# Two arrays in place of one for the sum of the experts' rows, in a graph and mixture-of-experts kernel

## What is computed

```
x = x + gnn0(layernorm(x))        # graph attention, 8 heads
x = x + ffn0(layernorm(x))        # 8 experts, each takes its 256 best nodes
x = x + gnn1(layernorm(x))        # mean over in-edges, two 512x512 products, silu
x = x + ffn1(layernorm(x))        # 64 experts, top 2 per node, plus a shared one

def ffn0(x_flat):                                  # E = 8, C = 256
    probs = softmax(x_flat @ Wr, axis=0)           # over the nodes
    vals, idx = top_k(probs.T, C)
    h = gelu(einsum('ecd,edf->ecf', x_flat[idx], W1) + b1[:, None, :])
    out_e = einsum('ecf,efd->ecd', h, W2) + b2[:, None, :]
    weighted = vals[..., None] * out_e
    return zeros_like(x_flat).at[idx.reshape(-1)].add(weighted.reshape(-1, D))
```

## Time and profile before

| What | Value |
|---|---|
| time, median of 3 runs | 2386.32 us (2380.95 to 2394.46) |
| profiled execution, its own time | 2389.54 us |
| its span, first to last instruction | 2387.8 us |
| mean granted TensorE clock | 0.941 |
| busy: PE, DVE, ACT, POOL | 84%, 59%, 43%, 43% of the span |
| moved by DMA | 537.31 MB, 225 GB/s over the span |

### The profile page before, as it was taken

The page is one execution under the profiler, slowest core; times in us unless marked ns, Lnnn a source line. Parts: engine busy times, 40 slices in busy tenths (PEclk is TensorE's granted clock), DMA queues, the critical chain, the costliest instruction groups (busy, mean ns, idle before and its releaser), DMA issues. The chain is left out here.

```text
span 2387.8 us, 35619 instructions
## 1 busy us (share of the span) xinstructions
PE 2007.8 (84%) x8691; PEld 1271.1 (53%) x8691; DVE 1417.0 (59%) x3001; ACT 1020.1 (43%) x3220; POOL 1021.7 (43%) x1046
## 2 busy tenths in 40 slices
PE   5857888888887725169999999897999999999998
PEld 4745667666665213124433444354346888888544
DVE  6646889888888662466666656577852222222343
ACT  2225777777776503456666556344001111111000
POOL 1037777777772404257777777300001111111331
PEclk9978999999999858679999999999999999999999
DMA  5648888888883735777777777785316999999652
GB/s 147 124 154 244 243 245 240 240 248 243 242 236 108 264 108 106 196 247 224 224 225 224 224 224 224 249 279 176 128 48 221 365 366 368 364 367 351 237 189 89
DMA packets 276215, 537.31 MB, mean 225 GB/s; under 512 B 43508, under 2 KB 121948, under 8 KB 275860
## 3 DMA queue, kind: packets, MB, share of 16 engines
q0 software_dynamic: 80544, 261.97, 37.9%
q1 hardware_dynamic: 177043, 240.65, 29.7%
q10 hardware_dynamic: 18464, 32.84, 4.2%
HBM read 449.56 MB, written 86.57 MB: 225 GB/s over the span
## 5 line engine op out<-in xcount | busy, mean ns | idle before, releaser
L852 POOL DMA_INDIRECT g_G<-tab,src_of_item x440 | 441.1, 1002 | 179.7 <-issue 106.7
L917 PE MATMUL g_psA<-g_G,g_oh 128*128 128x261 f32 x1760 | 443.0, 398 | 60.1 <-DVE g_G L1067 47.2
L1222 PE MATMUL g_psA<-g_G,g_oh 128*128 x832 | 386.0, 607 | 78.6 <-SPq L1178 69.5
L1162 POOL DMA_INDIRECT g_G<-tab,src_of_tile x392 | 370.7, 946 | 165.3 <-issue 84.1
L974 ACT ACTIVATE g_G<-g_G 128x64 f32<-128x64 f32 x1760 | 425.1, 336 | 0.0
L1265 DVE TENSOR_TENSOR acc<-acc,g_psA 128x512 f32 x416 | 285.5, 686 | 185.7 <-PE g_psA L1222 143.0
L917 PEld LDWEIGHTS g_psA<-g_G,g_oh 128*128 128x128 f32 x1760 | 326.7, 194 | 122.5 <-DVE g_G L1067 59.1
L1222 PEld LDWEIGHTS g_psA<-g_G,g_oh 128*128 128x128 f32 x832 | 147.3, 190 | 294.7 <-issue 293.8
L2427 PE MATMUL mo_bank<-mo_xT,mo_w 128*128 128x128 f32 x2304 | 269.1, 275 | 0.2 <-ACT mo_xT L2464 0.2
L2330 POOL DMA_INDIRECT mo_g<-tab,mo_slot x72 | 68.0, 945 | 456.9 <-PE mo_bank L2417 325.1
L2427 PEld LDWEIGHTS mo_bank<-mo_xT,mo_w 128*128 128x128 f32 x2304 | 263.0, 192 | 1.0 <-ACT mo_xT L2464 0.5
(11 more groups left out here) (421 smaller groups left out, 2524.4 us busy)
## 6 DMA issues: line engine op xcount, KB each, us to landing
mo_w<-in_L_ffn_w SPq DMA_DIRECT2D x216, 512.0 KB, 8.4
ys<-mo_y ACTq DMA_DIRECT2D x72, 256.0 KB, 5.6
g_ot<-reld SPq DMA_DIRECT2D x27, 512.0 KB, 5.9
ys<-sg_zeros SPq DMA_DIRECT2D x24, 512.0 KB, 4.2
g_G<-tab,src_of_item POOLq DMA_INDIRECT x440
g_pen<-pend SPq DMA_DIRECT2D x216, 32.0 KB
tab<-fi_row SPq DMA_DIRECT2D x25, 261.0 KB, 2.7
xmid<-at_x SPq DMA_DIRECT2D x25, 256.0 KB, 5.3
```

The costliest lines, as they stand in the source:

```text
L852: q.indirect_dma_start(G[:, j % RING, :], None, tab0, bass.IndirectOffsetOnAxis(K.src[:, j:j + 1], 0)).then_inc(gs[g % 3], 16)
L917: ins = tens.matmul(psA[u][:, f, 0:HW], oh[:, n % OR, h, :], G[:, r + h, f * HW:(f + 1) * HW], start=(h == 0), stop=(h == SUP - 1))
L1162: g.indirect_dma_start(G[:, (j + 1) % MR, :], None, table, bass.IndirectOffsetOnAxis(K.src1[:, j:j + 1], 0)).then_inc(got[j % MR], 16)
L1222: tens.matmul(psA[n % MB][:], oh[:, n % MO, :], G[:, ds(tile1 % MR, 1), :].rearrange("p o d -> p (o d)"), start=True, stop=True).then_inc( ...
```

## The change

The experts' rows are added into two arrays. Experts 0, 2 and 4 add into `xmid`, experts 1, 3, 5, 6 and 7 into a new array `xpart`, which `phase_route0` fills with zeros. Each array has its own chain of scatters with its own semaphore. `y` gets four buffers. SP loads the tiles of `xmid` when the first chain has landed, and the tiles of `xpart` through four buffers (`rest`) when the second has. POOL adds the two tile by tile, and VectorE's statistics wait for this (`joined`). `xmid` in memory keeps the first part alone, so `phase_sage` loads both arrays again for the residual, and POOL adds them there too (`whole`).

```diff
-def phase_route0(nc, K, lg, tab1, a, ew):
+def phase_route0(nc, K, lg, tab1, a, ew, xpart):
...
+        blank = p.sb("blank", [P, D])
...
         def _(g):
+            nc.gpsimd.memset(blank[:], 0.0).then_inc(blanked, 1)
             nc.gpsimd.iota(tio[:], [[1, NT], [0, E0]], base=0, channel_multiplier=0,
...
             loaded = ew.load(s, a, ws)
+            s.wait_ge(blanked, 1)
+            s.dma_start(xpart.rearrange("(t p) d -> p t d", p=P),
+                        blank[:].unsqueeze(1).to_broadcast([P, NT, D])).then_inc(bs, 16)
+            s.wait_ge(bs, 16)
             s.wait_ge(st, 16)
             s.wait_ge(ws, loaded)
...
-def phase_experts0(nc, K, a, tab1, xmid, ew, acc, tab2):
+def phase_experts0(nc, K, a, tab1, xparts, ew, acc, tab2):
...
+    YB = 4
+    ZB = 4
+    parts = ((0, 2, 4), (1, 3, 5, 6, 7))
+    part = [next(k for k in range(2) if e in parts[k]) for e in range(E0)]
+    rank = [parts[part[e]].index(e) for e in range(E0)]
...
-        y = p.sb("y", [P, 2, HC, D])
+        y = p.sb("y", [P, YB, HC, D])
+        rest = p.sb("rest", [P, ZB, D])
...
         def _(s):
-            s.wait_ge(sca, 16 * HC * E0)
+            s.wait_ge(sca[0], 16 * HC * len(parts[0]))
             for n in range(NT):
-                s.dma_start(xm[:, n, :], xmid[n * P:(n + 1) * P, :]).then_inc(xl[n], 16)
+                s.dma_start(xm[:, n, :], xparts[0][n * P:(n + 1) * P, :]).then_inc(xl[n], 16)
+            s.wait_ge(sca[1], 16 * HC * len(parts[1]))
+            for n in range(NT):
+                wait(s, joined, n - ZB + 1)
+                s.dma_start(rest[:, n % ZB, :], xparts[1][n * P:(n + 1) * P, :]).then_inc(rl[n % ZB], 16)
...
                 q.wait_ge(yr, HC * (e + 1))
-                if e:
-                    q.wait_ge(sca, 16 * HC * e)
+                k = part[e]
+                if rank[e]:
+                    q.wait_ge(sca[k], 16 * HC * rank[e])
                 for c in range(HC):
                     j = e * HC + c
-                    q.indirect_dma_start(xmid, bass.IndirectOffsetOnAxis(ix[:, j:j + 1], 0), y[:, e % 2, c, :], None,
-                                         bounds_check=NP - 1, compute_op=ALU.add).then_inc(sca, 16)
-            q.wait_ge(sca, 16 * HC * E0)
+                    q.indirect_dma_start(xparts[k], bass.IndirectOffsetOnAxis(ix[:, j:j + 1], 0), y[:, e % YB, c, :], None,
+                                         bounds_check=NP - 1, compute_op=ALU.add).then_inc(sca[k], 16)
+            for n in range(NT):
+                q.wait_ge(xl[n], 16)
+                q.wait_ge(rl[n % ZB], 16 * (n // ZB) + 16)
+                nc.gpsimd.tensor_tensor(xm[:, n, :], xm[:, n, :], rest[:, n % ZB, :], ALU.add).then_inc(joined, 1)
+            for k in range(2):
+                q.wait_ge(sca[k], 16 * HC * len(parts[k]))
...
-                    wait(v, sca, 16 * HC * (e - 1))
-                    nc.vector.tensor_tensor(y[:, e % 2, c, :], psY[c][:], b2[:, e, :], ALU.add).then_inc(yb, 1)
+                    if e >= YB:
+                        v.wait_ge(sca[part[e - YB]], 16 * HC * (rank[e - YB] + 1))
+                    nc.vector.tensor_tensor(y[:, e % YB, c, :], psY[c][:], b2[:, e, :], ALU.add).then_inc(yb, 1)
             for n in range(NT + 1):
                 if n < NT:
-                    v.wait_ge(xl[n], 16)
+                    v.wait_ge(joined, n + 1)
                     ln.stats(v, n, n % 2, xm[:, n, :])
...
-def phase_sage(nc, K, a, acc, own, xmid, tab3, ys, s13, s2, top, tix):
+def phase_sage(nc, K, a, acc, own, xmid, xpart, tab3, ys, s13, s2, top, tix):
...
+        xb = p.sb("xb", [P, XB, D])
...
             nc.gpsimd.memset(zeros[:], 0.0).then_inc(zr, 1)
+            for n in range(NT):
+                q_.wait_ge(xl[n % XB], 32 * (n // XB) + 32)
+                nc.gpsimd.tensor_tensor(xt[:, n % XB, :], xt[:, n % XB, :], xb[:, n % XB, :], ALU.add).then_inc(whole, 1)
...
                     s.dma_start(xt[:, n % XB, :], xmid[n * P:(n + 1) * P, :]).then_inc(xl[n % XB], 16)
+                    s.dma_start(xb[:, n % XB, :], xpart[n * P:(n + 1) * P, :]).then_inc(xl[n % XB], 16)
...
-                    v.wait_ge(xl[m % XB], 16 * (m // XB) + 16)
+                    v.wait_ge(whole, m + 1)
                     vv.tensor_tensor(acc[:, m, 0:D], sg[:, m % 2, :], xt[:, m % XB, :], ALU.add).then_inc(xd, 1)
```

More of the change, by code:

```diff
@@ L227, in build @@
     xmid = dram("xmid", [NP, D])
+    xpart = dram("xpart", [NP, D])
     tab1 = dram("tab1", [NP, D + E0])
@@ L256, in build @@
                 with ew:
-                    phase_route0(nc, K, lg, tab1, a, ew)
-                    phase_experts0(nc, K, a, tab1, xmid, ew, acc, tab2)
+                    phase_route0(nc, K, lg, tab1, a, ew, xpart)
+                    phase_experts0(nc, K, a, tab1, (xmid, xpart), ew, acc, tab2)
         best = sb("best", [P, NT, 8])
@@ L265, in build @@
                 phase_mean(nc, K, tab2, acc, a, own, s13, s2)
-                phase_sage(nc, K, a, acc, own, xmid, tab3, ys, s13, s2, best, tix)
+                phase_sage(nc, K, a, acc, own, xmid, xpart, tab3, ys, s13, s2, best, tix)
             phase_moe(nc, K, a, xmid, tab3, xsh, ys, own, s13, s2, best, tix, out)
@@ L1526, in phase_route0 @@
     with Phase(nc, "r0") as p:
+        blank = p.sb("blank", [P, D])
+        blanked = p.sem("blanked")
+        bs = p.sem("bs")
         pv = p.sb("pv", [P, 1])
@@ L1745, in phase_experts0 @@
     AHEAD = 4
+    YB = 4
[3 more added lines that the diff above has]
+    rank = [parts[part[e]].index(e) for e in range(E0)]
+    assert sorted(parts[0] + parts[1]) == list(range(E0))
     with Phase(nc, "e0") as p:
@@ L1751, in phase_experts0 @@
         hT = p.sb("hT", [F0, 2, CAP0])
-        y = p.sb("y", [P, 2, HC, D])
+        y = p.sb("y", [P, YB, HC, D])
+        rest = p.sb("rest", [P, ZB, D])
         ln = Norm(p, nc)
         normed = p.sem("normed")
+        rl = [p.sem(f"rl{q}") for q in range(ZB)]
+        joined = p.sem("joined")
         xl = [p.sem(f"xl{n}") for n in range(NT)]
@@ L1761, in phase_experts0 @@
         got = [p.gather_sem(f"got{e}") for e in range(E0)]; turned = p.sem("turned"); cop = p.sem("cop")
-        hd = p.sem("hd"); act = p.sem("act"); yd = p.sem("yd"); yb = p.sem("yb"); yr = p.sem("yr"); sca = p.gather_sem("sca")
+        hd = p.sem("hd"); act = p.sem("act"); yd = p.sem("yd"); yb = p.sem("yb"); yr = p.sem("yr"); sca = [p.gather_sem(f"sca{k}") for k in range(2)]
         b = p.block(K.counted)
@@ L1830, in _ @@
                     j = e * HC + c
-                    nc.scalar.activation(y[:, u, c, :], y[:, u, c, :], ACT.Copy,
+                    nc.scalar.activation(y[:, e % YB, c, :], y[:, e % YB, c, :], ACT.Copy,
                                          scale=g[:, j, D + e:D + e + 1]).then_inc(yr, 1)
@@ L1921, in phase_sage @@
         xl = [p.sem(f"xl{q}") for q in range(XB)]
+        whole = p.sem("whole")
         turned = p.sem("turned")
```

## The result

The changed kernel takes 2406.34 us (median of 5 runs, 2403.36 to 2408.47) against 2386.32; the ratio, taken over all runs, is 1.007, 95% interval 1.0055 to 1.0086. (The medians alone are 20.0 us apart; the five runs of before spread from 2380.95 to 2395.56.) It is slower, by more than the 0.5% that I had called the limit. The forecast was 2394.9 with a range of 2384 to 2406, and "same" had the largest chance: the sign of the sum was right, its size was half of what came. The median lies 0.3 us above the range; 2386.32 times the ratio, 2403.0, lies inside it. The profiled execution took 2406.47 us with a span of 2404.7, 16.9 us more than before.

The account below looks back on a forecast made before the run. Scatters of the experts' rows, then load, norm and store of the sum, were taken to bound this stretch; +5.0 (start) + 2.6 (norm) + 1.0 (sage) = +8.6 us on 2386.32 gave 2394.9, range 2384 to 2406.

Parts of the forecast that it names:

- same: Whole kernel: a time difference under 0.5%, 11.9 us; chance 0.63.
- The start: Start of the experts' norm statistics: later by 5 us, as loads of `xmid` meet the last experts' scatters.
- the one in which loads and scatters halve the engines: Under the last experts: pairs 5 and 6 take 4.2 us longer each, statistics start at 995.6, 4.9 us later.
- The case of exclusive engine time: Under the last experts: work ends at about 990 at best, statistics start at 994.2, 3.5 us later.
- Hidden after all: Under the last experts: other queues fill the scatters' waiting, start 3.6 us earlier, total 2386.3 us; chance 0.20.
- The norm: Experts' norm, 24 steps: 1.45 us per tile in place of 1.34, +2.6 us, bounds 0 and +10.5.
- The pace is the largest of three: Experts' norm, per tile: DVE 1.34 us, POOL 1.27 to 1.53, or the four-buffer ring, (1.53 + landing)/4.
- The ring sets the norm: Experts' norm: four `rest` slots with landings of 5.6 us set 1.78 us per tile, total 2402.8 us; chance 0.20.
- the sage case: Rival for sage: DVE loses a whole 1.27 us POOL add per tile, +11.7 us, total 2405.6 us; chance 0.08.
- Sage: Sage phase: loads covered, POOL adds meet DVE's two-input operations at +0.37 us each, mostly within slack; +1 us.
- The clearing of `xpart`: Before the first gather of expert rows: the 16.2 us fill runs on idle engines and costs nothing.
- the 5.1 us that two chains can win before the loads: Experts' scatters: undisturbed, the last lands at 982.8 against 987.9, since the chain's last three links stay in series.

Follow-up runs that it names:

- Experiments 5 and 7: 5: changed kernel, SP loads `xmid`'s tiles only after both chains landed, 1.0062; 7: kernel before plus 25 unused tile loads under the last three experts, 1.0018.
- experiment 8: Changed kernel without the load of `xpart` and POOL's addition in sage; ratio 1.0055, sage 148.68 us against 151.38.
- experiment 1: Changed kernel with the last VectorE instruction of a norm tile (L210) reading one tensor and a per-partition scalar instead of two tensors; ratio 1.0039.

## Why the prediction was right or wrong

**The start: right in mechanism, mis-sized.** The term was +5.0, measured +1.9. Of my cases I chose the one in which loads and scatters halve the engines and pairs 5 and 6 lose 4.2 us each. They lost 3.35 and 2.30. The case of exclusive engine time was the right one, and its sum could have been sharper: 959.7 + 28.8 = 988.5, where I had put 990, + 2.67 + 1.26 = 992.4, against 992.58. The addition took 1.26 us, not the 1.53 of a busy stretch. The Trainium skill, DMA: Bandwidth & Descriptors, "Issuing engines are not separate DMA queues", says that transfers started by different engines run on the same 16 DMA engines and interleave. Experiments 5 and 7 agree: steps of 8 us without the loads, 10.4 to 11.3 with them. The rival *Hidden after all* falls with this.

**The norm: the step that failed is "The pace is the largest of three".** It took DVE's own pace as "1.34 as now". None of the three was the limit: POOL did its 25 additions from 991.28 to 1025.8 and DVE did not wait for them after the first; the `rest` loads landed in 2.8/4.3/5.0 us (least, median, most; the median is the 4.3 that I had taken, between the rows), mostly below the 4.9 at which *The ring sets the norm* would decide, and eight buffers gained nothing. What grew was DVE's own time, through one operation of 128 numbers. I had the rule, weighed it, and applied it to sage's large operations only; I never listed which of DVE's small operations in the norm take two tensors. The list by line of one tile would have shown one, at 0.16 us, and its price beside an addition is up to 1.27: that is the bound that the term lacked. The measured 1.72 us per tile is near the ring rival's 1.78, from another cause; that the time came out beside the range's upper end, which the sage case had set, is luck.

**Sage: +1.0 taken, +3.7 measured**, of which experiment 8 gives 2.7 to the added load and addition. Meetings that hold DVE are rarer than one per tile, but one costs up to 1.08 us on DVE (1.76 against 0.68), not the 0.37 that I read from the median of the attend phase. The slack of 0.74 us per step does not hide that. And I had priced the two-input operations alone; L2134, with one tensor, was held as well. The rival *POOL holds DVE in sage* named the mechanism, and its time of 2405.6 is near the measured one, but for a place that holds a fifth of the loss.

**The rest.** The clearing of `xpart` cost nothing, as worked out; the first gather of expert rows starts within 0.2 us of before. The mean phase's +1.9 was in no case. One idle addition brings as much; why is open.

What could the change have won? With the hold removed (experiment 1) it is still 0.39% slower. The 10.0 us by which its trace is longer than before's lie, at the same marks, 2.1 in the start, 1.7 in the norm, 2.4 in the mean phase and 3.9 in sage. In the start, the second array adds 6.55 MB of loads, 16.2 us of full engines, in a stretch in which they were already busy for 0.54 of the time (957 to 988 us before); the 5.1 us that two chains can win before the loads don't pay for it. But most of the loss that is left comes from the places that the sum had at +1 and at nothing. That no order of these loads wins was argued here, not shown; the two that ran, early and late, end 0.8 us apart.

## What to carry to other kernels

Before giving POOL tile arithmetic beside VectorE, list every VectorE instruction in that stretch with two tensor inputs in SBUF, the 128x1 ones too, and price each at up to a whole POOL instruction. A form that takes one of them as a per-partition scalar escaped it here at 128x1 (214 ns each time, against a mean of 525), but at 128x512 an instruction of this form was held in sage (L2134, up to 1591 ns), so look at its time too. When DMA engines show a full share, add engine times; a full share at low bandwidth was no room here. And a split sum pays for its second array in every place that reads the sum.

## What the runs showed of the hardware that I had not expected

All of the program's gathers, those of the attend phase too, some 800 us ahead of the addition, take 941 or 942 ns at the least in the kernel before and 948 to 952 with one POOL addition in the experts' phase. So it does not come from what ran ahead of them in that execution; it goes with the program as a whole. Two kernels with 946 ns and two with 953 to 957 ran on the same chip. Neither 25 memsets there nor an addition in the attend phase does it, and a multiplication with a constant almost doesn't (947 to 949 at the median). Why stays open.

A pair of accumulating scatters (0.52 MB) is worth as much engine time as 1.7 MB of plain loads (4.2 us at 405 GB/s), and it keeps this price beside other traffic: 28.8 us full, 28.8 us by the sum.
